# An extra store buffer, later input loads and a reordered gate step in a three-phase recurrence and mixture kernel

## The reference, cut to what matters

```python
xn = _layernorm(x)                       # x: 8 x 2048 x 2048, float32
r = sigmoid(xn @ Wa.T + ba)
i = sigmoid(xn @ Wx.T + bx)
a = exp(-8 * softplus(-Lam) * r)
u = sqrt(1 - a**2) * (i * xn)
h[t] = a[t] * h[t-1] + u[t]              # scan over the tokens, per channel
probs = softmax(xn @ Wr.T + br)          # 8 experts
y = einsum(einsum(xn, A), B) / 64        # rank 64 per expert
out = x + h + y[argmax(probs)] * max(probs)
```

## Time and profile before

| what | us |
|---|---|
| two timed runs | 2142.46 and 2397.66 (median 2270.06) |
| profiled execution, its own time | 2143.65 |
| its span on the slowest core (core 5) | 2142.1 |
| phase 1, core 5, to the first matmul of phase 2 | 244.94 |
| phase 2, to the last of its matmuls | about 1597.7 |
| phase 3, first router matmul to the end | 1621.64 to 2142.1 |

### The profile page before, as it was taken

One profiled execution on the slowest core, in us unless ns is written; L12 is line 12 of the kernel. 1 busy time (PEld: TensorE's weight loads), 2 busy tenths in 40 slices (PEclk: granted clock), 3 DMA queues, 4 the chain that ended last, 5 costly groups with the idle time before them and its releaser, 6 DMA issues. The chain is left out here.

```text
span 2142.1 us, 21130 instructions; the slowest of 8 cores (2120.4 to 2142.1 us)
## 1 busy us (share of the span) xinstructions
PE 1853.1 (87%) x8448; PEld 870.2 (41%) x8448; DVE 535.1 (25%) x588; ACT 522.4 (24%) x430; POOL 293.6 (14%) x219
## 2 busy tenths in 40 slices
PE   3443699999999999969999999999984697888987
PEld 2343344444444444424444444444431243333433
DVE  4564111221131122111121131122112332222414
ACT  2332222422432342222422332242232100000000
POOL 0121110121111112111121111112103310000101
PEclk9766699999999999989999999999997798998989
DMA  6999823232232122151221122122006364361616
GB/s 169 273 261 286 232 79 99 79 97 61 60 91 67 50 69 79 30 147 50 66 82 50 50 77 71 50 69 79 30 10 193 93 163 132 101 195 44 192 40 197
DMA packets 233222, 228.10 MB, mean 106 GB/s; under 512 B 11778, under 2 KB 192132, under 8 KB 231076
## 3 DMA queue, kind: packets, MB, share of 16 engines
q1 hardware_dynamic: 109668, 107.20, 18.4%
q10 hardware_dynamic: 106560, 60.82, 10.7%
q0 software_dynamic: 16896, 58.73, 7.9%
HBM read 159.54 MB, written 67.11 MB: 106 GB/s over the span
## 5 line engine op out<-in xcount | busy, mean ns | idle before, releaser
L468 PE MATMUL pr<-xc2h,wrah 128*128 128x512 bf16 x1024 | 389.3, 380 | 34.4 <-DMA xc2l<-xpl 20.9
L471 PE MATMUL pr<-xc2l,wrah 128*128 128x512 bf16 x1024 | 389.2, 380 | 0.0
L474 PE MATMUL pr<-xc2h,wral 128*128 128x512 bf16 x1024 | 389.2, 380 | 0.0
L468 PE MATMUL pi<-xc2h,wrxh 128*128 128x512 bf16 x1024 | 389.1, 380 | 0.0
L471 PE MATMUL pi<-xc2l,wrxh 128*128 128x512 bf16 x1024 | 389.1, 380 | 0.0
L474 PE MATMUL pi<-xc2h,wrxl 128*128 128x512 bf16 x1024 | 389.1, 380 | 0.0
L91 ACT ACT_TABLE_LOAD x99 | 127.0, 1283 | 881.6 <-PE pi L474 814.4
L91 DVE TENSOR_TENSOR uub<-sfb,isb 128x1024 f32<-128x1024 f32 x32 | 39.2, 1226 | 1064.6 <-ACT sfb L91 1064.6
L599 POOL DMA_DIRECT2D yat<-isb x32 | 17.9, 560 | 1137.1 <-DVE isb L91 587.1
L583 POOL TENSOR_TENSOR wrxl<-wfx,wrxh 128x2048 bf16<-128x2048 f32 x31 | 158.5, 5114 | 43.0 <-ACT wrxh L91 42.4
L468 PEld LDWEIGHTS pr<-xc2h,wrah 128*128 128x128 bf16 x1024 | 100.4, 98 | 156.4 <-issue 36.5
(11 more groups left out here) (102 smaller groups left out, 1525.7 us busy)
## 6 DMA issues: line engine op xcount, KB each, us to landing
wfx<-wxT ACTq DMA_DIRECT2D x32, 1024.0 KB, 5.9
wfa<-waT SPq DMA_DIRECT2D x32, 1024.0 KB, 6.4
xr<-x SPq DMA_DIRECT2D x16, 1024.0 KB, 10.8
xfm<-XB ACTq DMA_DIRECT2D x16, 1024.0 KB, 22.6
yat<-isb POOLq DMA_DIRECT2D x32, 512.0 KB, 3.0
YA<-yat SPq DMA_DIRECT2D x64, 256.0 KB, 6.1
XF<-xfm SPq DMA_DIRECT2D x64, 256.0 KB, 8.4
out<-OT POOLq DMA_DIRECT2D x64, 256.0 KB, 8.0
```

The costliest lines, as they stand in the source:

```text
L468: tensor.matmul(dst, whk, rhs_h, start=first, stop=False, skip_group_check=True)
L471: tensor.matmul(dst, whk, rhs_l, start=False, stop=False, skip_group_check=True)
L474: mm = tensor.matmul(dst, wlk, rhs_h, start=False, stop=last, skip_group_check=True)
```

## The change

Three things change.

In phase 1 XB gets a third buffer and a third semaphore, so `xbev(j)` waits for the store of tile j-3. SP issues there only the loads of `xc2h0` and `xc2l` with k below 8: 12 instead of 24.

In phase 2 the other 12 loads are issued at the block's start: 4 of `xc2h0` (even k from 8) by SP ahead of its first `wfa`, and 4 of `xc2h0` and 4 of `xc2l` (odd k from 9) by ACT ahead of its first `wfx`. TensorE's wait at k = 8 is on three semaphores.

In phase 3, for tb = 0 alone, `hmm_group(0, 1)` stands between the two transposes, `hmm_group(0, 2)` takes its place behind the second, and gbc 0 to 3 follow each other with no group between. The first two `bt_casts` come behind the exponential. Four unused semaphores go.

```diff
-        XB = [sb1(f"XB{j}", [128, D]) for j in range(2)]
+        XB = [sb1(f"XB{j}", [128, D]) for j in range(3)]
@@
-                for k in range(NK):
-                    half = s_xc2[0] if k < 8 else s_xc2s[0]
+                for k in range(8):
                     sync.dma_start(xc2h0[:, ts(k, W2)],
-                                   xph[ts(k, 128), ts(0, W2)]).then_inc(half, 16)
+                                   xph[ts(k, 128), ts(0, W2)]).then_inc(s_xc2[0], 16)
@@
-                    if j >= 2:
-                        scalar.wait_ge(s_spx[j % 2], 16 * (j // 2))
-                    scalar.activation(XB[j % 2][:], ptB[:],
+                    if j >= 3:
+                        scalar.wait_ge(s_spx[j % 3], 16 * (j // 3))
+                    scalar.activation(XB[j % 3][:], ptB[:],
@@
             def _(sync):
+                for k in range(8, NK, 2):
+                    sync.dma_start(xc2h0[:, ts(k, W2)],
+                                   xph[ts(k, 128),
+                                       ts(0, W2)]).then_inc(s_xc2s[0], 16)
                 for idx2 in range(1, NIDX2):
@@
-                                tensor.wait_ge(s_xc2s[0], 192)
+                                tensor.wait_ge(s_xc2s[0], 64)
+                                tensor.wait_ge(s_xc2u, 128)
                                 tensor.wait_ge(s_xc2g2, 64)
@@
                 scalar = Ser(scalar, ssS, stS)
+                for k in range(9, NK, 2):
+                    scalar.dma_start(xc2h0[:, ts(k, W2)],
+                                     xph[ts(k, 128),
+                                         ts(0, W2)]).then_inc(s_xc2u, 16)
+                    scalar.dma_start(xc2l[:, ts(k, W2)],
+                                     xpl[ts(k, 128),
+                                         ts(0, W2)]).then_inc(s_xc2u, 16)
@@
                     if tb != 0:
                         hmm_group(tensor, tb, 0)
+                    else:
+                        hmm_group(tensor, 0, 1)
                     tensor.wait_ge(s_g3, tb + 1)
@@
-                    hmm_group(tensor, tb, 1)
+                    hmm_group(tensor, tb, 1 if tb != 0 else 2)
                     gbc_mm(tensor, tb, 0)
                     gbc_mm(tensor, tb, 1)
-                    hmm_group(tensor, tb, 2)
+                    if tb != 0:
+                        hmm_group(tensor, tb, 2)
                     gbc_mm(tensor, tb, 2)
@@
-                    if tb == 0:
-                        for i in range(2):
-                            bt_casts(i)
                     scalar.wait_ge(s_ls, tb + 1)
                     scalar.activation(EXt[:], LSt[:], AF.Exp).then_inc(s_sex, 1)
                     if tb == 0:
-                        for i in range(2, 8):
-                            if i <= 5:
+                        for i in range(8):
+                            if 2 <= i <= 5:
                                 bt_odd_dma(i + 2)
                             bt_casts(i)
```

More of the change, by code:

```diff
@@ L171, in build_nc @@
     s_xc2gs = sem("s_xc2gs")
-    s_xc2t = sem("s_xc2t")
     s_xc2t2 = sem("s_xc2t2")
+    s_xc2u = sem("s_xc2u")
     s_xc30 = sem("s_xc3p0")
@@ L205, in build_nc @@
         s_cpX = sem("s_cpX")
-        s_cpXV = sem("s_cpXV")
         s_hic = sem("s_hic")
@@ L209, in build_nc @@
         s_sp = [sem(f"s_sp{j}") for j in range(2)]
-        s_spx = [sem(f"s_spx{j}") for j in range(2)]
+        s_spx = [sem(f"s_spx{j}") for j in range(3)]
         def fm_dst(base_h, m):
@@ L245, in _ @@
                                        xpl[ts(k, 128),
-                                           ts(0, W2)]).then_inc(half, 16)
+                                           ts(0, W2)]).then_inc(s_xc2[0], 16)
             @blk.scalar
@@ L274, in xbev @@
                     scalar.dma_start(fm_dst(xfm_h, j),
-                                     XB[j % 2][:]).then_inc(s_spx[j % 2], 16)
+                                     XB[j % 3][:]).then_inc(s_spx[j % 3], 16)
                 for m in range(NM):
@@ L370, in _ @@
                     gpsimd.wait_ge(s_sp[j], 32 * (NM // 2))
-                    gpsimd.wait_ge(s_spx[j], 16 * (NM // 2))
+                for j in range(3):
+                    gpsimd.wait_ge(s_spx[j], 16 * len(range(j, NM, 3)))
     with ExitStack() as ph:
@@ L658, in build_nc @@
         s_apd = [sem(f"s_apd{j}") for j in range(4)]
-        s_apc = sem("s_apc")
         s_aps = sem("s_aps")
@@ L664, in build_nc @@
         s_btd = [sem(f"s_btd{j}") for j in range(2)]
-        s_btc = sem("s_btc")
         s_bts = sem("s_bts")
```

## The result

The changed kernel takes 2123.34 us (median of 11 runs, lowest 2113.37) against 2145.92 us for the kernel before (10 runs). The ratio is 0.9895, 95% interval 0.9869 to 0.9921: 1.05% faster, where 1.3% was forecast. The profiled execution took 2119.94 us, with a span of 2118.4 us on core 0, which is its slowest.

The account below looks back on a forecast made before the run. Full DMA engines were taken to bound phase 1, TensorE's matmuls phase 2, and waits around the gates to cost time in phase 3. 2143.65 - 12.5 (phase 1) - 15.7 (phase 3) = 2115.4 us; 8-in-10 range 2099 to 2134.

Parts of the forecast that it names:

- 12 loads fewer and the third XB: Phase 1: 11.1 us saved by 3.15 MB fewer, 1.4 by the third buffer; together 12.5 us, between 6 and 16.
- signs of being wrong: Phase 1 shrinking by under 6 or over 16 us, or phase 3's spreads more than 5 us apart.
- The first rival: Phase 1: XB waits hide a poor transfer rate, the third buffer raises it; 2100 to 2106 us, chance 0.12.
- Phase 2 at no cost: Phase 2: the moved loads land before k = 8, and weights, about 10 us later, stay covered; cost 0.
- the second rival: Phase 2: a slow burst makes TensorE wait 12.5 us at k = 8, returning phase 1's gain; 2128 us, chance 0.14.
- The third rival: Phase 1: the deeper store queue delays loads of x, 56 us lost; 2171 us, chance 0.04.
- The exponential earlier: Phase 3, tb = 0: the exponential starts 2.9 us earlier, all on the path; later casts cost 0.
- POOL beside DVE's chain: Phase 3, tb = 0: DVE's chain from SM to Gt gets 1.5 us shorter, bounds 0 and 6.2.
- Group 1 in the gap: Phase 3: group 1's 48 matmuls take 10 us within TensorE's wait for the gates, leaving some 5 us of waiting.
- Four spreads in a row: Phase 3: four successive spreads, steps 3.23 us apart; first spread to output products 28.3 us, 11.3 us less.

Follow-up runs that it names:

- late_only: The kernel before with only the 12 loads moved to phase 2's start, XB with two buffers: ratio 0.9982, phase 1 233.7 us.
- late_again: The same kernel as late_only, executed a second time for its phase 1: phase 1 at 230.4 us, no ratio.
- xb3_only: The kernel before with only the third XB buffer: ratio 0.9997, phase 1 237.7 us.
- late4: The changed kernel with six loads more (k = 4 to 7) moved to phase 2's start: ratio 0.9868 to the kernel before, phase 1 225.9 us.
- exp_only: The kernel before with only the earlier exponential: logits' transpose to output products 70.0 us against 70.6, no ratio.
- pe_only: The kernel before with only TensorE's new order in phase 3: logits' transpose to output products 59.5 us against 70.6, no ratio.
- hold: The changed kernel with POOL's subtractions of B waiting until the gates exist: ratio 0.9935 to the kernel before.
- gate_only: The kernel before with only the phase 3 changes: ratio 0.995, logits' transpose to output products 58.8 us against 70.6.
- spread_hold: The kernel hold with bt_casts 5, 6, 7 each behind one of hgh(0), hgh(1), hgh(2): ratio 0.9923 to the kernel before.
- combo: late4 and hold, group 3 between spreads 1 and 2, bt_casts 4 to 7 behind hgh(1): 2107.61 us, ratio 0.9829 to the kernel before.

## Why the prediction was right, and where it was off

The forecast was 2115.4 us, the measurement 2123.34, inside the range of 2099 to 2134; by ratio 0.9868 against 0.9895. The direction and the two places of the gain were right. The gain was 22.6 us instead of 28.2.

*12 loads fewer and the third XB.* That bytes over a full DMA system set phase 1 held. The sum of 12.5 us was too high: the four executions with phase 1 as before have a mean of 239.2 us, the five with both parts 226.0 to 232.6, mean 229.3: 9.9 us. The 13.3 in the first table, close to the forecast, was luck. The mis-sized term is 11.1 us for the twelve loads, which brought some 8.4 (9.9 less 1.5; by themselves, in late_only and late_again, 7.1); the third buffer has 1.5 (1.4 forecast, but hardly outside the scatter). The 8.4 us lie near the lower bound of 7.8, which takes the loads at the fastest rate seen. I had priced them at the share of time of SP's queue. What the traces show, as means over the cores from 180 us to the start of phase 2: the DMA share is 0.94 in the four kernels and 0.94 in the five, so the engines are not emptier without the loads, but the rate is 266 GB/s in the four and 254 in the five. The loads that left were cheaper by the byte than what stayed. Why they are was not tried.

*Two of the signs of being wrong came.* On core 5 phase 2 begins at 227.5 us, below the 229 to 239 stated, and phase 1 shrank by 17.4 us there, over the 16 stated. The step that failed is to read this sign off one core: before, the eight cores begin phase 2 anywhere from 231.6 to 244.9 us, and core 5 was the last of them. And the spreads are not all under 5 us apart: the third begins 5.66 us behind the second on core 0, and over 5 us on five of the eight cores (8.52 on core 7). That is the exponential's step, below.

*The first rival* (the waits for XB hide a poor rate) is refuted by xb3_only: no wait left, the time the same. The waits moved to ACT's issues.

*Phase 2 at no cost, and the second rival.* Right: no wait at k = 8, weights 30.0 us into the phase for 28 forecast, phase 2 within 0.5 us. late4 shows that even 18 loads fit.

*The third rival* (x delayed by a deeper queue) did not come: DVE's wait for x on core 5 is 22.2 us for 25.2, nearly all of it one wait.

*The exponential earlier.* Here a step failed, "all of that is on the path" (2.9 us), and "the casts come 0.3 us later [...] cost 0". It was on the path only to the first spread. I had looked for who needs the casts' results, and they are needed late; but the casts themselves stand ahead of `hgh` in ACT's order, and their own end is set by transfers that an earlier exponential does not hasten. exp_only shows it alone: -3.0 and +2.8 us. In the changed kernel the same shows as 30.0 us from the first spread to the output products instead of the 27.4 of pe_only.

*POOL beside DVE's chain.* 1.5 us forecast, and nothing came: the chain's median is 8.34 us for 7.96 before. That PRt loses its excess was right (0.19 us on every core), but the excess reappears at PMt. The 2.7 us from the logits' to the gates' transpose, for 4.4 forecast, are about the exponential's 2.9 and nothing else. The 10.5 us that I started from are those of core 5, the longest chain of the eight. The bounds of 0 and 6.2 us were right: the changed kernel stands at the lower one, and hold takes all of the excess.

*Group 1 in the gap.* Right. The gates' transpose waits 2.84 us on core 0 (2.8 to 5.5 over the cores) for the 5 forecast, and behind it group 2 takes 13.0 us as before (13.2), with the slow restart.

*Four spreads in a row.* 11.3 us forecast, 12.2 in pe_only where nothing holds `hgh`. The difference to the 9.6 of the changed kernel belongs to the exponential's step. The fetches of GR2 were in time in pe_only, where the spreads follow each other as forecast.

In sum: phase 1 with 9.9 us and phase 3 with 11.1 to 12.5 us (pe_only 11.1, gate_only 11.8, the changed kernel 12.5) make 21 to 22.4 us, close to the 22.6 of the two medians.

## What to carry to other kernels

Where the transfer engines are full, count bytes: an additional buffer mostly moves the wait, here from the buffer to the issue, and moving transfers to a stretch with idle DMA time pays, here 8.4 of the 11.1 us at which their queue's share priced them. Where an operation is brought forward on an engine that works in order, list what now stands between it and the next operation that someone waits for, with the transfers those wait for, not only who uses their results. Compare a stretch over all cores, not one core with another: a single core's phase 1 and gate chain differed by more than the change. Fill an engine's gap first and then look at what the work was covering at its old place.

## What the runs showed of the hardware that was not expected

The chain of small DVE operations from SM to Gt (4.35 us without company) took 6.2 to 10.5 us beside POOL's subtractions, and the time falls on whichever operations are under way: PRt 2.02 us before, the seven PMt 5.79 us after, none in hold.

A short pause of TensorE can cost its clock, and does not always. On core 0 after, the granted clock is 0.50 (1.2 GHz) right behind the pause of 2.84 us ahead of the gates' transpose, after 1.00 during group 1:

```profile
1655.00:1657.00 2.00, 1.78 (x6) 0.90 (x8) 0.68 (x1) 1.36 (x3) 2.00 (x3) 0.50 0.48 118
```

From there to the first spread, over group 2, it takes 12.2 us. Seven of the eight cores are like this (pauses of 2.84 to 5.53 us, 12.2 to 13.7 us behind them). Core 7 kept its clock across 3.31 us and took 10.9:

```profile
1636.91 0.60 PE L816 MATMUL pY<-identf,Gt 128*8 128x128 f32 x4 [3.31 <-DVE Gt L91]
1636.00:1638.00 2.00, 1.09 (x8) 0.68 (x9) 0.76 (x4) 1.24 (x2) 1.23 (x2) 1.00 0.50 107
```

Core 4 of gate_only lost it behind 2.23 us, core 0 of spread_hold kept it across 2.55. In hold and combo, with pauses of 1.62 us at most, all cores take 10.9 us. So a pause of this kind costs up to about 3 us behind it, or nothing.

Pairs of cores fall behind the others in the output stage by nearly as much as the whole change is worth (22.6 us), and not always the same ones. Behind the output products of tb = 0, cores 0 and 1 of gate_only took 378.6 and 381.3 us and the other six 361 to 366; in spread_hold it was cores 4 and 5, with 382.6 and 385.0 (the others 363 to 372). Since the metric is the slowest core, such a pair sets it. Why was not tried.
